# A top-64 attention layer in which the 64th value is picked one section later, from sorted values held twice, with new instruction sequences for VectorE and TensorE

## The reference, cut to what matters

```
scores = jnp.einsum('bhqd,bhkd->bhqk', q, k) / np.sqrt(DHEAD)
scores = jnp.where(causal_mask[None, None], NEG_INF, scores)
topk_vals, _ = jax.lax.top_k(scores, TOP_K)
threshold = topk_vals[..., -1:]
scores = jnp.where(scores < threshold, NEG_INF, scores)
weights = jax.nn.softmax(scores, axis=-1)
out = jnp.einsum('bhqk,bhkd->bhqd', weights, v)
...
x = x + _L1_attn_ref(xn, ...) + _L1_ffn_ref(xn, ...)
```

## Time and profile before

| | |
|---|---|
| median of 3 runs | 2473.63 us (2472.95 to 2478.28) |
| the profiled execution, its own time | 2477.97 us |
| its span, first to last instruction | 2476.2 us |
| mean granted TensorE clock | 0.872 of full |
| DVE busy in the span | 67% |
| PE, ACT, POOL busy in the span | 77%, 57%, 23% |

### The profile page before, as it was taken

One profiled execution on the slowest core, in us unless ns is written; L12 is line 12 of the kernel. 1 busy time (PEld: TensorE's weight loads), 2 busy tenths in 40 slices (PEclk: granted clock), 3 DMA queues, 4 the chain that ended last, 5 costly groups with the idle time before them and its releaser, 6 DMA issues. The chain is left out here.

```text
span 2476.2 us, 36312 instructions
## 1 busy us (share of the span) xinstructions
PE 1915.1 (77%) x10415; PEld 1113.4 (45%) x10448; DVE 1652.1 (67%) x3759; ACT 1400.3 (57%) x2883; POOL 573.0 (23%) x1478
## 2 busy tenths in 40 slices
PE   6678777799997896888567787777787847787776
PEld 3333333357775443555334444444444424444444
DVE  4566566621114465767488888888898878788874
ACT  2255555543331421323477877877778747877873
POOL 0011111100001440000233333333423423333340
PEclk7699999999995997999878888888977878888977
DMA  6000000010001220000200000100100000000000
GB/s 194 20 17 13 16 16 13 10 35 1 0 0 43 77 94 1 0 0 0 54 15 22 27 18 23 26 14 26 27 13 26 27 13 13 27 16 24 18 18 10
DMA packets 38262, 62.40 MB, mean 25 GB/s; under 512 B 10225, under 2 KB 15347, under 8 KB 38004
## 3 DMA queue, kind: packets, MB, share of 16 engines
q1 hardware_dynamic: 38069, 60.51, 8.3%
HBM read 34.14 MB, written 17.83 MB: 21 GB/s over the span
## 5 line engine op out<-in xcount | busy, mean ns | idle before, releaser
L1451 ACT ACTIVATE a_trash<-a_sc,a_search 128x1024 bf16<-128x1024 f32 (+7 forms) x768 | 585.6, 768 | 52.8 <-DVE a_sc L1560 20.2
L1262 PE MATMUL a_ps_o<-a_kT,a_v 128*65 128x512 f32 (+3 forms) x768 | 335.7, 542 | 128.2 <-DVE g_x L1616 113.6
L1229 PE MATMUL a_ps_s<-a_k,a_q 128*128 128x512 f32 (+3 forms) x768 | 323.4, 533 | 42.0 <-DVE a_sc L1560 28.3
L1246 PE MATMUL a_ps_t<-g_ident,a_sc 128*128 128x128 f32 x1152 | 276.5, 322 | 4.9 <-ACT a_short L1461 4.9
L1468 ACT ACTIVATE a_kT<-a_ps_t 128x512 f32<-128x512 f32 x288 | 169.1, 587 | 186.1 <-PE a_ps_t L1248 186.1
L1560 DVE TENSOR_SCALAR_CACHE_REDUCE a_sc<-a_ps_s,g_search 128x1024 f32<-128x1024 f32 (+7 forms) x256 | 208.3, 814 | 84.0 <-PE a_ps_s L1231 69.1
L479 DVE TENSOR_REDUCE a_top<-a_ps_row 128x1 f32<-128x512 f32 (+3 forms) x384 | 196.5, 553 | 93.9 <-PE a_ps_row L366 60.1
L1248 PE MATMUL a_ps_t<-a_minus,a_short 128*128 128x128 bf16 x1152 | 257.6, 248 | 0.0
L461 ACT ACTIVATE a_prob<-a_ps_col 128x1024 f32<-128x1024 f32 (+7 forms) x256 | 159.9, 653 | 156.2 <-PE a_ps_col L423 96.9
L1246 PEld LDWEIGHTS a_ps_t<-g_ident,a_sc 128*128 128x128 f32 x1152 | 193.9, 168 | 97.3 <-issue 66.5
L1534 DVE SCALAR_TENSOR_TENSOR a_below<-a_sc,a_found 128x640 f32<-128x640 f32 (+7 forms) x256 | 212.6, 841 | 0.0
(11 more groups left out here) (257 smaller groups left out, 3321.5 us busy)
## 6 DMA issues: line engine op xcount, KB each, us to landing
a_v<-g_v SPq DMA_DIRECT2D x32, 260.0 KB, 2.3
q1turned<-p_full SPq DMA_DIRECT2D x32, 256.0 KB, 2.0
a_q<-q1turned SPq DMA_DIRECT2D x32, 256.0 KB, 3.8
a_k<-k1turned SPq DMA_DIRECT2D x32, 256.0 KB, 4.3
stack<-p_parts SPq DMA_DIRECT2D x24, 256.0 KB, 3.8
a_q<-stack SPq DMA_DIRECT2D x32, 96.0 KB, 2.2
a_k<-stack SPq DMA_DIRECT2D x32, 96.0 KB, 2.2
le_w<-d_w SPq DMA_DIRECT2D x1, 2048.0 KB, 8.7
```

The lines of the kernel that those rows point to most:

```text
L1229: pe.matmul(ps_s[:, j % 2, c:c + w], q[:, p, i * P:width], k[:, p, c:c + w], start=True, stop=True)
L1246: pe.matmul(out, columns(h, i)[:, c * P:(c + 1) * P], g.ident[:, :], is_transpose=True, start=True, stop=False)
L1262: m = pe.matmul(ps_o[0:VW1, lo // HALF, (lo % HALF) * P:CH], v[:, p, c, :], kT[:, u % 2, a * P:b * P], start=(c == 0), stop=(c == LAST[lo ...
L1451: act.activation(trash[:, u % 2, 0:(i + 1) * P], columns(h, i), ACT.Sign, scale=-1.0, bias=trials[:, p, c, i:i + 1], accum_out=balance[:, ...
```

## The change

`pick` for a head moves from the end of POOL's section to the next one, where it stands behind `tally` and ahead of the seed and `place`. So that the sorts of the next head can go on, `sorted` gets a second half, and `place`, which overwrites `hit`, waits for the verdict. The verdict's matmul moves from PE's place ahead of its last `weigh` to the head of PE's next section, on the other bank. DVE's section now starts with `found`, and flags follow marks 0, 2 and 4. The order of PE, of DVE's marks, sorts, keeps and leaves is new. No instruction of the arithmetic is added or taken away.

```
-        FIRST, FINAL = 4, 5
+        FIRST, FINAL = 0, 2
...
-        sorted_ = r.sb("sorted", [P, TB, NB])
+        sorted_ = r.sb("sorted", [P, 2, TB, NB])
...
@@ tensor, section
+                    if gating:
+                        pe.wait_ge(verdict_ready, n - 1)
+                        pe.matmul(ps_t[0:1, odd, 0:TB], g.ones[:, 0:1], verdict[:, :], start=True, stop=True).then_inc(flag_back, 1)
+                    if leaving:
+                        project(n - 3, 0)
...
+                        project(n - 3, 4)
                     if ahead:
                         scores(n + 1, i2, p1, 2)
                     if leaving:
-                        for t in range(6):
-                            project(n - 3, t)
+                        project(n - 3, 5)
+                    if gating:
+                        turn(n - 2, h + 2, odd + 0, 0)
                     if ahead:
                         scores(n + 1, i2, p1, 3)
                     if leaving:
                         project(n - 3, 6)
                         project(n - 3, 7)
...
+                        turn(n - 2, h + 2, odd + 1, 1)
+                        scores(n + 1, i2, p1, 4)
+                        turn(n - 2, h + 2, odd + 2, 2)
+                        weigh(*head, odd + 0, 0)
+                        turn(n - 2, h + 2, odd + 3, 3)
+                        weigh(*head, odd + 1, 1)
+                        scores(n + 1, i2, p1, 5)
...
-                            pe.wait_ge(verdict_ready, n)
-                            pe.matmul(ps_t[0:1, 1 - odd, 0:TB], ...
...
@@ gpsimd
 def place():
+                        wait(pool, verdict_ready, n - 1)
...
 def pick():
-                        wait(pool, cutoff_ready, n - 1)
-                        pool.wait_ge(sorted_ready, n)
-                        ... sorted_[:, :, :]
+                        wait(pool, cutoff_ready, n - 2)
+                        pool.wait_ge(sorted_ready, n - 1)
+                        ... sorted_[:, p1, :, :]
...
                         tally()
+                    if gating:
+                        pick()
...
                         second_move()
-                    if sorting:
-                        pick()
@@ vector, order of a section (k = keep_scores, m = mark, s = sort, l = leave, sh = shares)
-k0 k1 find flags m4 judge cut_off m3 m5 sh0 sh1 l0 l1 k2 m1 s40 m0 s30 s41 s31 m7 sh2 l2
-k3 m2 s42 s20 s32 s21 m6 s70 s22 k4 s71 s10 s72 s11 s60 s50 s61 k5 s12 s00 s51 s01 s62
-k6 s02 k7 s52
+find k0 m0 m2 m4 flags judge cut_off m5 m6 sh0 sh1 k1 l0 s50 k2 m1 sh2 m3 l1 s00 l2
+k3 s20 m7 s10 s21 s01 k4 s40 s70 k5 s11 s41 s71 s60 s30 k6 s31 s42 s72 s61 s02 s62 s51
+k7 s52 s12 s32 s22
```

More of the change, by code:

```diff
@@ L1295, in section @@
                         project(n - 3, 7)
-                    odd = h % 2
                     if gating:
-                        turn(n - 2, h + 2, odd, 0)
                         turn(n - 2, h + 2, odd + 1, 1)
-                    for x in range(TU):
-                        if sorting and x == TU - 1:
-                            pe.wait_ge(verdict_ready, n)
[L1303 to L1312, removed]
+                    if ahead:
+                        scores(n + 1, i2, p1, 4)
@@ new lines, in section @@
+                    if gating:
[3 more added lines that the diff above has]
+                        weigh(*head, odd + 1, 1)
+                    if ahead:
+                        scores(n + 1, i2, p1, 5)
+                    if gating:
+                        weigh(*head, odd + 2, 2)
+                        turn(n - 2, h + 2, odd + 4, 4)
+                    if ahead:
+                        scores(n + 1, i2, p1, 6)
@@ new lines, in section @@
+                    if gating:
+                        weigh(*head, odd + 3, 3)
+                        turn(n - 2, h + 2, odd + 5, 5)
+                    if ahead:
+                        scores(n + 1, i2, p1, 7)
+                    if gating:
+                        weigh(*head, odd + 4, 4)
+                        turn(n - 2, h + 2, odd + 6, 6)
+                        weigh(*head, odd + 5, 5)
+                        turn(n - 2, h + 2, odd + 7, 7)
+                        weigh(*head, odd + 6, 6)
+                        turn(n - 2, h + 2, odd + 8, 8)
+                        weigh(*head, odd + 7, 7)
@@ L1314, in _ @@
+                    if late:
+                        scores(n + 2, i4 * 2 + (h + 2) // 2, 1 - p1, 0)
+                    if gating:
+                        weigh(*head, odd + 8, 8)
+                    if late:
+                        scores(n + 2, i4 * 2 + (h + 2) // 2, 1 - p1, 1)
                 pe.wait_ge(blank, 3)
@@ L1422, in section @@
                         after(made[0])
+                    if gating:
+                        pick()
+                    if made[0]:
+                        after(made[0])
                     if ahead:
@@ L1646, in section @@
                         shares(1)
+                    if ahead:
+                        keep_scores(1)
+                    if leaving:
                         leave(0)
-                        leave(1)
+                    if sorting:
+                        sort(5, 0)
                     if ahead:
@@ L1652, in section @@
                         mark(1)
[L1653 to L1658, removed]
                     if leaving:
                         shares(2)
+                    if sorting:
+                        mark(3)
+                    if leaving:
+                        leave(1)
+                    if sorting:
+                        sort(0, 0)
+                    if leaving:
                         leave(2)
@@ L1693, in section @@
                     if sorting:
+                        sort(3, 1)
+                        sort(4, 2)
+                        sort(7, 2)
+                        sort(6, 1)
                         sort(0, 2)
+                        sort(6, 2)
+                        sort(5, 1)
                     if ahead:
@@ L1698, in section @@
                         sort(5, 2)
+                        sort(1, 2)
+                        sort(3, 2)
+                        sort(2, 2)
                     if made[0]:
```

61 lines of the change are left out of this document (30 added, 31 removed).

## The result

The changed kernel is slower by 0.3%. Its median is 2484.49 us over 8 executions (2478.98 to 2486.53), against 2475.59 for the kernel before in the same sessions; the ratio is 1.0031 with an interval of 1.0020 to 1.0042. A second measurement gave 1.0026 (1.0015 to 1.0036). I had forecast 10.6 us less, and it is some 8 us more.

The account below looks back on a forecast made before the run. Bound: the 37.43 us loop of last sort, `pick`, `tally`, `found`, flags, branch, cutoff and DVE's work. 26 tails at -0.47 and five branches back at +0.32 make -10.6: 2473.6 to 2463.0 us, range 2441 to 2490.

Parts of the forecast that it names:

- the tail from E to C: From end of last sort (E) to cutoff (C): flags at E + 4.25 instead of 4.72, 0.47 us less a section.
- The bound of E + 4.60: Latest flags time in ordinary sections, if each mark beside `pick` is also held, as mark 4 is by line 1360.
- my last counts: ACT's last count ends at E - 2.0 to E - 3.2, so `tally` (1.4 us) ends before E.
- rival (c): POOL: ACT's last count stays late, so `tally` delays `pick`; +0.6 us a section, 2491 us; chance 0.17.
- nothing here is late: DVE's work from C to E: PE delivers everything in time, with 0.3 us to spare in the last case.
- the branch back: At the loop's backward branch DVE sets the loop: flags at E + 5.51, 0.32 us later, five times.
- the ends, and the gap: Last cutoff's tail taken as unchanged; flags to cutoff also unchanged, at 3.91 us.
- Rival (b): No measurable change: marks wait for `pick`'s steps, or the gap from flags to cutoff changes; 2469 to 2478 us; chance 0.20.

Follow-up runs that it names:

- second profile: The changed kernel run once more, unaltered, for another profile: 2483.6 us, ratio 1.0026 to the kernel before.
- short body: Changed kernel with the search of tiles 1 to 7 left out behind its branch: 2402.35 us; the kernel before with the same cut: 2376.00 us.
- the two repairs of the order: Changed kernel with shares(2) moved behind leave 1 and marks 0, 2 and 4 moved behind flags: 2435.46 us, ratio 0.9847.

## Why the prediction was wrong

**Right: the tail from E to C.** I put flags at E + 4.25 in ordinary sections, 0.47 earlier than before. They came at 4.20 and 4.27, with three steps of `pick` held by the three marks, and at 3.42 once the marks lay behind flags. One count was off: `pick` has nine instructions and not ten, and when the marks ended six were done and three left, not two. The bound of E + 4.60 asked that the marks be held as well, and they were not: mark 4 took 0.88 us, where it took 1.13 beside line 1360. `tally` ended 1.7 to 2.6 us before E, where my last counts put it 0.6 to 1.8 before, so rival (c) did not happen in the steady sections. It did at the ends. Ahead of the second cutoff `tally` ended 0.5 us after E. And near the end, before the last cutoff but one, `tally` ran from 2405.57, after the last sort had ended at 2404.3, and that section took 34.6 instead of 33.4 us.

**Wrong: "nothing here is late".** The step that failed is the one on what DVE needs from PE. I let shares 2 fall due at C + 6.9 and put `project(7)` at "C + 5.7 at full clock and C + 7.0 at half". In the trace it ended at C + 7.8 at half clock: `scores(3)` started behind keep 1 at C + 4.25, took 2.5 us and its mask, and the two projections 1.2. At full clock `project(7)` ended at C + 6.2. So both of my times were early, by 0.8 and 0.5 us, and even my own C + 7.0 lay behind the due time of C + 6.9, which contradicts "nothing here is late". Half clock was not the exception that I took it for: `scores(3)` began in it in 18 of 27 stretches. PE now stands idle ahead of the verdict and of the gates. I had named exactly this idle time, but only under (c), as something that makes ACT late. Worth: 0.5 to 0.6 us a section on the mean (14.8 and 16.9 us in the two profiles), 0.8 where it struck, and 20 us of time when it was taken away.

The kernel with shares 2 later measured 2463.31 us, and my forecast was 2463.0. That agreement is partly luck, since the terms below were not in my sum and happen to cancel.

**Mis-sized: the branch back.** I wrote 0.32 us, five times. Flags came 1.0 later there, since the first reduction after the jump started at E + 2.7 to 3.7 and not at E + 2.4. It was 2.7 or more in all kernels whose section starts with `found`, and 2.3 to 2.6 in those that start with keep 0; the reason was not looked for. The gap behind them then fell by 1.3, so these tails as a whole changed by -0.3.

**Not in the sum: the ends, and the gap.** The gap from flags to the cutoff fell by 0.27 in ordinary sections, 6 us in my favour that I had set at nothing. At the ends, the time from the first cutoff to the second and the one to the last but one got 1.7 and 1.3 us longer and the last one 0.4 shorter (second profile), which I had put down as if they were the same. The second profile has 2.8 us more before the first cutoff and 2.1 more behind the last. These are hardly the change's: 2.6 of the 2.8 lie before layer 1's first keep (1199.27 before, 1201.87 there, 1199.72 in the first profile), and the first profile has only 0.1 more behind the last cutoff. All of them together are 7.5 us in the second profile.

The parts of the second profile against before add up: tails to flags 23 x -0.42 = -9.7 and 5 x 1.00 = +5.0; gaps 22 x -0.27 = -5.9 and 5 x -1.28 = -6.4 (the section with the search is left out); C to E 23 x 0.56 + 5 x 0.39 = +14.8; the ends +7.5. The sum is +5.3, and the spans differ by 4.8 (the means are rounded). From the first cutoff to the last the kernel before takes 1179.2 us and both profiles after take 1179.1. So between the cutoffs the gains that I forecast, and those that I had not, are used up by the longer work from C to E. The rest of the difference between the medians lies in executions of which there is no profile, and stays open.

**Rival (b)** held a point that I used too little: that "the gap from flags to cutoff changes with the new sequence". It was 3.94 and 4.52 us in two kernels with mark 4 in it, 3.67 with nothing in it, 3.70 with three marks, and 1.04 with a short body. The Trainium skill's rule on taken branches to a target outside two pages ("Runtime: NRT & Kernel Launch", "Instruction fetch mechanics") fits these runs; no row shows the fetch, and where the pages lie was not read out. What the runs show is that the body's length makes the gap: the search as a loop kept all eight inner branches, and the time from the branch's record to the cutoff still fell to 0.9 us, with queued marks filling it. That it is a fetch is argued.

## What to carry to other kernels

When work is moved to open a gap on one engine, ask which clock TensorE will have in the work that now follows its new idle time, and set the due time of every reader against the slow case; a reader that costs nothing to move later is the cheap remedy. When an engine's idle time ends in "issue" ahead of an instruction behind a branch, measure it with a shorter body before touching anything else: here the loop in the body was worth 50 us, and the two repairs of the order together 44 to 48. Measure again afterwards, since a shorter gap also brings every later due time forward: with the short body the changed order lost to the old one by some 25 us. If the idle time has to stay, put the instructions that hold another engine's work into it, not ahead of it.

## What the runs showed of the hardware that I had not expected

- At a branch over a body of 137 VectorE instructions in the source, the next instruction of DVE came 2.4 to 4.9 us after the branch's record ended, and 0.16 us after it over a body of 18 (from the flags on: 3.6 to 6.0 us, and 1.0). In one kernel the same code cost 1.6 us more in the next section, and the difference came back in each round of the loop.
- At the loop's backward branch DVE's first instruction came 2.3 to 2.6 us after the last one where a section starts with keep 0, and 2.7 to 3.7 where it starts with `found`.
- After idle time, PE's matmuls ran at 1.2 GHz in two sections of three: `scores(3)` took 2.50 us, and 1.35 at 2.4 GHz. With matmuls that nothing reads in the idle time it took 1.30.
- A POOL step that is held by a mark goes through when the mark ends, though another mark is queued. The marks ended at 1560.60, 1561.13 and 1561.93, and the three steps 0.06 to 0.12 us behind them, stretched by 0.16 to 0.51 us. The marks were not longer: 0.35, 0.61 and 0.88 us.
